# A mixture-of-experts tile loop: fetch depth, order on PE, bias rows and register loads changed together

## The reference

```python
t = x * rsqrt(mean(x * x) + EPS) * scale
vals, idx = top_k(t @ gate_w.T + gate_b, 4); w = softmax(vals)
# for each of the 4 experts e of a token:
h = t @ mlp1_w[e].T + mlp1_b[e]            # 256 -> 512, even columns glu, odd columns lin
s = min(glu, 7) * sigmoid(1.702 * min(glu, 7)) * (clip(lin, 7, 7) + 1)
y = s @ mlp2_w[e].T + mlp2_b[e]            # 256 -> 256
out = x + gate * sum_e w_e * y_e
```

## Time and profile before

| | us |
|---|---|
| runs of the kernel before: median (lowest to highest) | 1270.71 (1267.17 to 1271.97), 3 runs |
| the profiled execution's own time | 1259.12 |
| its span, first to last instruction | 1257.4 |
| mean granted clock of TensorE over the span | 0.949 |
| PE / DVE / ACT / POOL busy | 1115.0 / 791.6 / 637.7 / 528.7 |

### The profile page before, as it was taken

The page is one execution under the profiler, slowest core; times in us unless marked ns, Lnnn a source line. Parts: engine busy times, 40 slices in busy tenths (PEclk is TensorE's granted clock), DMA queues, the critical chain, the costliest instruction groups (busy, mean ns, idle before and its releaser), DMA issues. The chain is left out here.

```text
span 1257.4 us, 22022 instructions
## 1 busy us (share of the span) xinstructions
PE 1115.0 (89%) x7283; PEld 941.3 (75%) x7283; DVE 791.6 (63%) x1998; ACT 637.7 (51%) x1733; POOL 528.7 (42%) x642
## 2 busy tenths in 40 slices
PE   4899999999999999999999999999875688888870
PEld 3688888888888888888888888888664577767660
DVE  2646667776776777676677766776555444445547
ACT  2534655646565555655556565555423444444440
POOL 1613344444344443434444343443422365656640
PEclk9999999999999999999999999999966698999995
DMA  4310101000000000000000000000401122222229
GB/s 138 115 47 5 34 5 34 17 25 18 4 17 6 17 17 9 18 4 17 8 14 17 9 18 5 18 1 5 136 12 63 42 85 76 84 78 84 85 76 287
DMA packets 39566, 54.96 MB, mean 44 GB/s; under 512 B 8186, under 2 KB 31434, under 8 KB 39458
## 3 DMA queue, kind: packets, MB, share of 16 engines
q1 hardware_dynamic: 27540, 31.86, 8.2%
q0 software_dynamic: 9328, 18.83, 4.9%
q10 hardware_dynamic: 2592, 2.88, 0.7%
HBM read 40.05 MB, written 13.49 MB: 43 GB/s over the span
## 5 line engine op out<-in xcount | busy, mean ns | idle before, releaser
L662 POOL TENSOR_TENSOR prob<-prob,rinv 112x750 f32<-112x750 f32 x128 | 185.1, 1446 | 373.6 <-DVE rinv L1104 373.5
L738 ACT ACTIVATE prob<-ps_s,negmax 112x375 f32<-112x375 f32 x256 | 144.4, 569 | 237.3 <-DVE negmax L1099 233.6
L1110 DVE TENSOR_TENSOR pT_lo<-ps_pt,pT_hi 125x672 fp32r<-125x672 f32 x128 | 109.6, 856 | 74.5 <-ACT pT_hi L824 74.5
L1179 PE MATMUL ps_kv<-ctxT_hi,wkv 128*128 128x376 f32 x512 | 141.3, 357 | 7.7 <-DVE v_lo L895 3.6
L1099 DVE TENSOR_REDUCE negmax<-ps_s 112x2 f32<-112x750 f32 x128 | 118.9, 929 | 0.3
L895 DVE TENSOR_TENSOR v_lo<-ps_kv,v_hi 125x512 fp32r<-125x512 f32 x96 | 66.3, 691 | 76.3 <-ACT v_hi L728 76.3
L1179 PE MATMUL ps_kv<-wkv,ctxT_hi 128*125 128x512 f32 x384 | 111.5, 412 | 1.4 <-DVE k_lo L891 1.4
L1331 PE MATMUL ps_pt<-ident,prob 112*125 112x112 f32 x768 | 104.6, 273 | 1.3 <-POOL prob L662 1.3
L1460 POOL DMA_INDIRECT places<-ysb,place_i x71 | 70.6, 995 | 74.4 <-ACT ysb L1489 59.8
L824 ACT ACTIVATE pT_hi<-ps_pt 125x672 fp32r<-125x672 f32 x128 | 93.5, 730 | 9.2 <-PE ps_pt L1331 1.0
L1331 PEld LDWEIGHTS ps_pt<-ident,prob 112*125 112x125 f32 x768 | 94.7, 190 | 1.7 <-POOL prob L662 1.7
(11 more groups left out here) (266 smaller groups left out, 2678.0 us busy)
## 6 DMA issues: line engine op xcount, KB each, us to landing
zb<-places SPq DMA_DIRECT2D x16, 448.0 KB, 13.5
arena<-in_L_ffn_mlp_w SPq DMA_DIRECT2D x24, 256.0 KB, 4.5
ctx_in<-in_ctx SPq DMA_DIRECT2D x16, 375.0 KB
acc<-in_L_xattn_w_kv SPq DMA_DIRECT2D x4, 512.0 KB, 12.6
stage_w<-in_L_ffn_mlp_w SPq DMA_DIRECT2D x8, 256.0 KB, 3.1
x_in<-in_x SPq DMA_DIRECT2D x16, 112.0 KB, 2.0
normed_rows<-row SPq DMA_DIRECT2D x16, 112.0 KB, 1.8
out<-acc ACTq DMA_DIRECT2D x16, 112.0 KB, 7.6
```

Source lines behind the costliest of these rows:

```text
L662: e_prob.done(eng.tensor_tensor(prob[0:TQ, p % 2, :, :], prob[0:TQ, p % 2, :, :], rinv[:, 2 * p:2 * p + 2].unsqueeze(2).broadcast_to([TQ, ...
L738: e_exp.done(eng.activation(prob[0:TQ, p % 2, half, :], S[0:TQ, half, 0:SK], ACT.Exp, bias=negmax[:, h:h + 1], accum_out=rowsum[:, h:h + 1]))
L1110: e_pt_lo.done(eng.tensor_tensor(pT_lo[:, :, :, :].rearrange("p h k t -> p h (k t)"), PT[0:KEYT, :, 0:NKEY * TQ], pT_hi[:, :, :, :].bitcas ...
L1179: last = eng.matmul(out_, lhs(i, k), rhs(j, k), start=(n == 1), stop=(n == KT * len(PASSES)))
```

## The change

It does four things in `phase2`. XB goes from 6 to 10 and AHEAD from 5 to 9, so nine gathers are issued ahead. PE's turn becomes XT(i), H(i-1), Y(i-4), ST(i-2): Y stands behind H, a turn later than before, and ST behind Y, next to the XT of the following turn; ACT and DVE do the split of s (now i-3) first in their turn, and the loops have TILES + 4 turns. The bias product has 128 rows: `one` and `b1_r` are filled with zeros on POOL, then `one`'s first two rows with ones, and ACT's copy of the bias writes rows 0 and 1 after the fill. PE loads the expert numbers of twelve tiles with one call, every twelve turns (71 tiles: six calls).

```diff
--- before.py
+++ after.py
@@ -43,8 +43,9 @@
 LISTS = 256
 PLACE, WEIGHT, TOKEN = range(3)
 PLACES = B * TQ * TOPK
-XB, YB = 6, 3
-AHEAD = 5
+XB, YB = 10, 3
+AHEAD = 9
+GROUP = 12
 
 AT_WEIGHTS = tuple(range(20, 44, 2))
 N_EARLY = len(AT_WEIGHTS)
@@ -163,7 +164,7 @@
                 ("ysb", YB, D, F32), ("zsum", 2, 2 * D, F32))}
         arena = sb("arena", [128, 8 * 1024])
         with ExitStack() as place:
-            b1_r = sb("b1_r", [2, NE * HID], F32R, place)
+            b1_r = sb("b1_r", [128, NE * HID], F32R, place)
         stage_w = sb("stage_w", [128, 4 * 1024])
 
 
@@ -1384,7 +1385,7 @@
 
         t("w_e_room", [128, NE * 4 * KT * HID])
         w1, w2 = ([w_e[:, :, n + i, :, :] for i in range(2)] for n in (0, 2))
-        one = t("one", [2, 128], F32R)
+        one = t("one", [128, 128], F32R)
         need = t("need", [128, NE, NE])
         n_e, tiles, base = (t(name, [128, NE]) for name in ("n_e", "tiles", "base"))
         past = t("past", [128, 2, NE])
@@ -1437,7 +1438,10 @@
 
         @block.gpsimd
         def _(eng):
-            eng.memset(one[:, :].bitcast(F32), 1.0).then_inc(f_one, 1)
+            eng.memset(one[:, :].bitcast(F32), 0.0)
+            eng.memset(b1_r[:, :].bitcast(F32), 0.0).then_inc(f_one, 1)
+            eng.wait_ge(f_one, 1)
+            eng.memset(one[0:2, :].bitcast(F32), 1.0).then_inc(f_one, 1)
             eng.wait_ge(f_sent, 16 * TOPK * B)
             eng.wait_ge(s_plan, 2)
             eng.indirect_dma_start(listed[0:TILES, :, :].rearrange("p n k -> p (n k)"), None, entries[:, :],
@@ -1465,23 +1469,24 @@
             for n in range(N_EARLY, NE):
                 weights_high(eng, n)
             eng.wait_ge(f_b1, 16)
-            eng.activation(b1_r[:, :], b1_f, ACT.Copy).then_inc(f_b1_in, 1)
+            eng.wait_ge(f_one, 1)
+            eng.activation(b1_r[0:2, :], b1_f, ACT.Copy).then_inc(f_b1_in, 1)
             eng.wait_ge(s_list, 1)
             eng.activation(weight[:, :], ps_list[:, WEIGHT * TILES:(WEIGHT + 1) * TILES], ACT.Copy
                            ).then_inc(s_lists, 1)
-            for i in range(TILES + 3):
+            for i in range(TILES + 4):
+                j = i - 3
+                if 0 <= j < TILES:
+                    c_st.wait_ge(eng, j + 1)
+                    c_shi.done(eng.activation(sT_hi[:, j % 2, :], ST[j % 2], ACT.Copy))
                 if i < TILES:
                     c_xt.wait_ge(eng, i + 1)
                     c_xhi.done(eng.activation(xT_hi[:, i % 2, :], XT[i % 2], ACT.Copy))
-                j = i - 2
-                if 0 <= j < TILES:
-                    c_st.wait_ge(eng, j + 1)
-                    c_shi.done(eng.activation(sT_hi[:, j % 2, :], ST[j % 2], ACT.Copy))
                 j = i - 1
                 if 0 <= j < TILES:
                     c_u.wait_ge(eng, j + 1)
                     c_sg.done(eng.activation(sg[:, j % 2, :], u[:, j % 2, :], ACT.Sigmoid, scale=ALPHA))
-                j = i - 3
+                j = i - 4
                 if 0 <= j < TILES:
                     c_y.wait_ge(eng, j + 1)
                     if j >= YB:
@@ -1534,7 +1539,12 @@
             eng.wait_ge(s_lists, 1)
             eng.tensor_copy(token_i[:, :], ps_list[:, TOKEN * TILES:(TOKEN + 1) * TILES])
             eng.tensor_copy(place_i[:, :], ps_list[:, PLACE * TILES:(PLACE + 1) * TILES]).then_inc(s_lists, 1)
-            for i in range(TILES + 3):
+            for i in range(TILES + 4):
+                j = i - 3
+                if 0 <= j < TILES:
+                    c_shi.wait_ge(eng, j + 1)
+                    c_slo.done(eng.tensor_tensor(sT_lo[:, j % 2, :], ST[j % 2], sT_hi[:, j % 2, :].bitcast(F32),
+                                                 ALU.subtract))
                 if i < TILES:
                     c_xhi.wait_ge(eng, i + 1)
                     c_xlo.done(eng.tensor_tensor(xT_lo[:, i % 2, :], XT[i % 2], xT_hi[:, i % 2, :].bitcast(F32),
@@ -1543,13 +1553,6 @@
                 if 0 <= j < TILES:
                     c_h.wait_ge(eng, j + 1)
                     c_u.done(eng.tensor_scalar(u[:, j % 2, :], H[j % 2], LIMIT, None, ALU.min))
-                j = i - 2
-                if 0 <= j < TILES:
-                    c_shi.wait_ge(eng, j + 1)
-                    c_slo.done(eng.tensor_tensor(sT_lo[:, j % 2, :], ST[j % 2], sT_hi[:, j % 2, :].bitcast(F32),
-                                                 ALU.subtract))
-                j = i - 1
-                if 0 <= j < TILES:
                     c_sg.wait_ge(eng, j + 1)
                     c_st.wait_ge(eng, j - 1)
                     c_s.done(eng.scalar_tensor_tensor(s_f[:, j % 2, :], u[:, j % 2, :], LIMIT + 1.0,
@@ -1576,14 +1579,17 @@
                                      ident[0:TILES, 0:TILES])
             last.then_inc(s_list, 1)
             eng.wait_ge(f_b1_in, 1)
-            eng.wait_ge(f_one, 1)
+            eng.wait_ge(f_one, 2)
             eng.wait_ge(s_owner, 1)
             eng.wait_ge(s_lists, 2)
             c_wlo.wait_ge(eng, 2 * NE)
             expert = {}
-            for i in range(TILES + 3):
+            for i in range(TILES + 4):
                 if i < TILES:
-                    expert[i] = eng.value_load(owner_i[0:1, i:i + 1], min_val=0, max_val=NE - 1)
+                    if i % GROUP == 0:
+                        _, loaded = nc.values_load_multi_w_load_instructions(
+                            owner_i[0:1, i:i + GROUP], engines=[mybir.EngineType.PE], min_val=0, max_val=NE - 1)
+                        expert.update(zip(range(i, i + GROUP), loaded))
                     eng.wait_ge(f_x[i % XB], 16 * (i // XB + 1))
                     c_xlo.wait_ge(eng, i - 1)
                     for k in range(KT):
@@ -1604,15 +1610,7 @@
                                               w1[c][:, own, k, :].rearrange("p e n -> p (e n)"), start=False,
                                               stop=(n == len(PASSES) - 1 and k == KT - 1))
                     c_h.done(last)
-                j = i - 2
-                if 0 <= j < TILES:
-                    c_s.wait_ge(eng, j + 1)
-                    c_slo.wait_ge(eng, j - 1)
-                    for m in range(HT):
-                        last = eng.transpose(ST[j % 2][:, m * 128:(m + 1) * 128],
-                                             s_f[:, j % 2, m * 128:(m + 1) * 128], ident[:, :])
-                    c_st.done(last)
-                j = i - 3
+                j = i - 4
                 if 0 <= j < TILES:
                     own = bass.ds(expert[j], 1)
                     c_slo.wait_ge(eng, j + 1)
@@ -1625,6 +1623,14 @@
                                               w2[c][:, own, m, :].rearrange("p e n -> p (e n)"), start=(n == 1),
                                               stop=(n == HT * len(PASSES)))
                     c_y.done(last)
+                j = i - 2
+                if 0 <= j < TILES:
+                    c_s.wait_ge(eng, j + 1)
+                    c_slo.wait_ge(eng, j - 1)
+                    for m in range(HT):
+                        last = eng.transpose(ST[j % 2][:, m * 128:(m + 1) * 128],
+                                             s_f[:, j % 2, m * 128:(m + 1) * 128], ident[:, :])
+                    c_st.done(last)
 
 
 # ---- launch: one core; inputs and outputs as the reference has them ----
```

## The result

| | before | after |
|---|---|---|
| runs: median (range, number) | 1268.41 us (1264.12 to 1271.97, 7) | 1257.01 us (1253.74 to 1263.02, 7) |
| ratio | | 0.992, interval 0.9893 to 0.9947 |
| profiled execution: time, span | 1259.1, 1257.4 | 1256.43, 1254.7 |
| first and last scatter | 1001.1, 1221.7 | 1006.0, 1220.9 |

The account below looks back on a forecast made before the run. The ring was taken as the loop's bound, then POOL's 2.57 us a tile: first scatter 1003.0, plus 154.2, then the last tile's way out and 4 us give last scatter 1176.8, 45 us less: 1226 us, range 1211 to 1249.

Parts of the forecast that it names:

- The step that failed: Tile loop: ring latency sets 3.27 us a tile; with six tiles a round, POOL's 2.57 us becomes the bound.
- the ring: Tile loop: ysb, its scatter, the next gather, PE, ysb again; 9.5 us a round for three tiles, 3.17 a tile.
- Rival 1: Tile loop: PE's late completions stay, coming with dense PE work; 17 us of 45 lost, 1243 (1229 to 1270); chance 0.22.
- the late "done": PE's completion of the ST turns reaches ACT 2.6 us late in the tile loop.
- The remark on rows 7: PE's queue: the next expert number is loaded at 1035.7, where the lateness begins; called a coincidence of times, not proof.
- Fetching nine ahead: POOL's gathers: deeper fetch removes the ring as bound, 1.6 us a tile against POOL's 2.57; four extra early gathers hidden.
- Bias over 128 rows: PE's bias product: full rows remove 0.38 us a tile, from 2.38 to 2.0 us.
- Rival 2: PE's bias product: the edit brings nothing, PE keeps 2.38 us a tile; 1239, or 1255 with dear loads; chance 0.12.
- Group loads: PE's queue: 4 us per twelve-number load, bounds 2.3 and 7.2; 0.7 us shows at first, 3.3 us stops at five others.
- Order: PE's turn: the new order bears 1.4 us of a late completion and delays the first Y by 1.0 us.
- Fills: POOL's new zero fills before the loop: cost 0 to 0.5 us, taken as 0.2.
- Clock: PE in the loop: full clock except 1.4 us more for a tile's worth behind each of five load stops.

Follow-up runs that it names:

- h3_narrow: g4_direct with an extra indirect gather of 64 bytes a row, which no tile reads, in place of each gather taken out: 1261.16 us, ratio 0.9981.
- h4_ahead: The kernel before with only the fetch depth changed (ten xg buffers, nine gathers ahead), on chip 8: 1260.46 us, ratio 0.9986.
- e1_ahead: The kernel before with only the fetch depth changed (ten xg buffers, nine gathers ahead), on chip 2: 1214.04 us, ratio 0.9943.
- i2_after: The kernel after, unchanged, run on chip 13: 1214.73 us, ratio 0.9934 to the kernel before.
- f1_after: The kernel after, unchanged, run on chip 14: 1257.36 us, ratio 0.9965 to the kernel before.
- e2_bias2: The kernel after with the bias back on 2 rows, on chip 2: 1228.77 us, ratio 1.0034 to the kernel before.
- f3_ahead_bias: The kernel before with the deeper fetch and the 128-row bias, old order and single loads, on chip 14: 1257.17 us, ratio 0.9965.
- f4_group: The kernel before with the group loads alone, on chip 14: 1269.67 us, ratio 1.0053.
- f2_single: The kernel after with one register load a tile again, on chip 14: 1252.05 us, ratio 0.9921 to the kernel before.
- h1_pause: f2_single with a POOL fill of 128x384 behind each scatter, on chip 8: 1250.09 us, ratio 0.9902 to the kernel before.
- g4_direct: The kernel after with the gathers from tile 10 on as plain DMAs on SP's queue, on chip 7: 1219.49 us, ratio 0.9631.
- h2_busy: g4_direct with a POOL fill of 128x1408 in place of each gather taken out, on chip 8: 1221.53 us, ratio 0.9677.

## Why the prediction was wrong

- **The step that failed** is the first: "the rest of the 3.27 us is latency round a ring", with "once round carries six tiles. Even at 9.5 us that is 1.6 us a tile, under POOL's 2.57". The time round is kept by held completions. In the 9.5 us of the earlier trace rows POOL issues six DMAs too, from 1170.33 to 1178.35, and then stands 1.47 us, and the chain itself has a piece that rows 4 leave out:

```profile
1176.06 0.38 ACT xT_hi L1475
1176.45 1.84 another core or an unknown queue
```

There ACT waits until 1178.29 for an ST that PE had ended at 1176.34. The time from the first scatter to the sixtieth after it was forecast at 154.2 us and measured at 195.5: 41 of the 44 us by which the last scatter (1220.9 for 1176.8) missed. h3_narrow has the same 9.5 us with indirect gathers that no tile waits for; h4_ahead, the depth alone, brings 0.14%, 2 us, where the step promised 45. That a ring of waits adds up to the pace doesn't show that the ring sets it. The sign was in the earlier trace rows: PE waited 17.6 us for xg, POOL 59.8 us for ysb, and the deeper fetch shortens the first alone, of which 4.3 us are the wait for the very first gather (load at 986.9, turns at 990.2).
- **Rival 1 came nearest**, at 0.22: the late "done" stays. Its reason was wrong and its price too low. It put the lateness down to dense PE work; in e1_ahead and i2_after PE works as densely and nothing is late. It took the hold as a fixed 2.6 us, of which the new order bears 1.4. But the lateness grows along POOL's run, to 3.8 us, so the 1.4 us of slack are used up. Measured per three tiles: 9.4 us against POOL's 7.7, 1.7 us and not 0.7. Over 20 threes that is 34 of the 41 us; the other 7 go with shorter runs (7 of four issues beside 15 of six) and the stops at group loads. The first scatter came 3 us later than forecast (1006.0 for 1003.0), and the last ten tiles took what was forecast for them, 19.4 us against 19.6. The result lies in that rival's range (1229 to 1270), which the range given cut off at 1249.
- **The remark on rows 7** set loads beside lateness. It was coincidence, as it had said it might be: with six loads the holds stay (f1_after).
- **Fetching nine ahead**: it removed the wait for xg, and on chips 2 and 13 it lets POOL run at its floor. The sum for that case holds: from the first gather to the last scatter 189.4 us forecast (987.4 to 1176.8), 188.2 us measured in e1_ahead and 189.9 in i2_after. What was wrong even there is the kernel before: without holds it takes 1222, so the depth is worth 0.6%.
- **Bias over 128 rows**: right, 2.38 to 1.99 us a tile, and it is the bias's doing: e2_bias2 with the new order has 2.37, f3_ahead_bias with the old one 1.98. Rival 2 gave 2.38. The Trainium skill (TensorE: Matmul & The Clock Gate, LDWEIGHTS) says that a load of few rows takes the same time as one of 128, and the traces agree, 0.18 us and 0.19; what failed is the prediction's step from the load's time to the tile's pace. Of the 0.39 us, 0.18 lie between XT and the bias, 0.11 between the bias and H, 0.10 in the next four products (the earlier trace rows against the tile above); by what mechanism, no run shows. It was worth 12 us beside the group loads (e2_bias2, i2_after); without them it can't be told from nothing where completions are held (f3_ahead_bias 0.9965, h4_ahead 0.9986, intervals overlapping).
- **Group loads**: taken at 4 us, measured 4.3 to 4.6; the five stops in the loop, taken at 3.3 us, were 2.2 to 3.8. That the bounds of 2.3 and 7.2 us met in the right place is part luck: the load was put at half of the time and is a fifth. What was missed is that the old loads cost almost nothing, hidden under PE's queue, so grouping is a loss: 7 us in f4_group, 5.3 us between f1_after and f2_single. Twelve numbers by the 200 ns a register of the Trainium skill (Runtime: NRT & Kernel Launch, Instruction fetch mechanics), which it gives beside the register loads of a kernel's launch, would be 2.4 us for the load, an estimate; here, out of SBUF, it is 0.86 us, and the cost is in the operations behind it.
- **Order**: it was to bear 1.4 us of a late completion at a price of 1.0 us. f3_ahead_bias against f2_single puts its gain at 5.1 us where completions are held, about what the intervals can tell.
- **Fills**: taken at 0.2 us, measured at none.
- **Clock**: the forecast took the full level but for a tile's worth behind each load. It fell to 0.84 between 1135 and 1207, where PE is busy for 55 of 72 us and stops up to 2.6 us at a hold and 2.2 and 2.5 at the two groups. In that stretch PE still stands idle 17 us, so it was hardly the clock that decided; no run separates it.

On chip 14 and chip 7 the change without its group loads is the best of the kernels that compute the whole result: 1252.05 against 1257.36 and 1262.69 (f2_single, after, before), and 1251.18 against 1266.22. Nothing here was found that keeps both the gathers and their order and is free of the holds.

## What to carry to other kernels

Before a ring of buffers is made deeper, look which engine stands at the break: if the consumer of that ring (here PE for xg) waits far less than the producer waits for something else, the depth is not what is missing. Where several completions of one engine are taken in one moment, look what another engine has just stopped doing. Take the kernel before and the changed one on the same chip: one program differed by 3.5% between chips. A register load that lies hidden under a full queue is cheaper one at a time than in a group that stops the queue.

## What the runs showed of the hardware

- **Completions of PE held while POOL issues indirect DMAs densely**: up to 3.8 us late in the kernel after, 4.4 in h1_pause. With breaks of 0.3 and 0.6 us between issues they come out singly and later and later, the rest together 0.5 to 1.2 us after the last issue. With one issue every 2.2 us (g4_direct) or 2.4 us (h2_busy, breaks of 1.45 us) nearly none is late. 64 bytes a row do it as well as 1 KB; plain DMAs of as many bytes from SP's queue and a busy POOL don't. ACT's and DVE's own completions are on time in the same traces (none of 207 and 213 in the loop of the kernel after).
- **Not on every chip**: of the five named chips three had it and two not, with the kernel before at 1263 to 1266 and at 1222 to 1223, a difference of 3.5%, larger than any change tried here that keeps the result. Why chips differ, and by what path POOL's issuing reaches PE's semaphores, no run shows.
- **A 2-row operand loaded into PE** among 128-row ones costs 0.39 us more than one of 128 rows that are mostly zeros, though its load is no longer (0.18 and 0.19 us).
- **Register loads**: one 0.30 us, twelve at once 0.86 us, and for each register 0.15 us of register operation and 0.02 us of assertion on top.
